# Eight rank-one products a batch in the low-rank layer become two products over four partitions

## The reference

```python
lt = x[:, 1:17, :]                      # sixteen tokens of each batch
even, odd = lt[:, ::2, :], lt[:, 1::2, :]
m1 = (even[:, :4, :, None] * odd[:, :4, None, :]).reshape(B, 512, 128)
m2 = (even[:, 4:, :, None] * odd[:, 4:, None, :]).reshape(B, 128, 512)
h = x @ W1.T + scale * einsum('bsd,bhd->bsh', x, m1) + b1
h = gelu(h)
out = h @ W2.T + scale * einsum('bsh,boh->bso', h, m2) + b2
```

## Time and profile before

| | |
|---|---|
| three timed executions | 821.05, 825.11 and 826.53 us, median 825.11 |
| the profiled execution | 825.88 us, of which the span from the first to the last instruction is 824.1 us |
| TensorE (PE) busy | 712.8 us (86%), mean granted clock 0.915 of full speed |
| VectorE (DVE) busy | 619.5 us (75%) |
| ScalarE (ACT), GpSimd (POOL) busy | 409.3 us, 394.3 us |
| fillers `ps_y<-zero_bf` within TensorE's time | 119.5 us |

### The profile page before, as it was taken

One profiled execution on the slowest core, in us unless ns is written; L12 is line 12 of the kernel. 1 busy time (PEld: TensorE's weight loads), 2 busy tenths in 40 slices (PEclk: granted clock), 3 DMA queues, 4 the chain that ended last, 5 costly groups with the idle time before them and its releaser, 6 DMA issues. The chain is left out here.

```text
span 824.1 us, 12171 instructions
## 1 busy us (share of the span) xinstructions
PE 712.8 (86%) x4422; PEld 423.6 (51%) x4422; DVE 619.5 (75%) x1083; ACT 409.3 (50%) x832; POOL 394.3 (48%) x475
## 2 busy tenths in 40 slices
PE   5468988997899888998899889997999889986867
PEld 2234545455645655555655655555655555554324
DVE  1277077998879866986989887988899778953692
ACT  1212633954397245843378248824682448433532
POOL 5543132694178413853269324962493018501671
PEclk9565999999999989996999999999999898967899
DMA  5321211431045101521054103520262114100410
GB/s 136 79 99 47 83 42 34 170 109 65 9 170 160 46 0 35 203 89 58 9 162 150 32 33 101 155 87 35 67 184 69 58 42 150 34 1 0 155 57 8
DMA packets 41241, 66.40 MB, mean 81 GB/s; under 512 B 8041, under 2 KB 30398, under 8 KB 38846
## 3 DMA queue, kind: packets, MB, share of 16 engines
q1 hardware_dynamic: 39006, 64.58, 24.4%
q10 hardware_dynamic: 2176, 1.05, 0.4%
HBM read 57.68 MB, written 7.86 MB: 80 GB/s over the span
## 5 line engine op out<-in xcount | busy, mean ns | idle before, releaser
L586 POOL TENSOR_TENSOR shared<-u,bcrow 128x512 f32<-128x512 f32 x128 | 203.6, 1620 | 64.1 <-DMA bcrow<-bc_dram 34.3
L963 DVE TENSOR_TENSOR_SCAN shared<-ps_f,shared 128x512 f32<-128x512 f32 x128 | 151.1, 1208 | 11.8 <-ACT ps_f L733 7.1
L865 DVE TENSOR_REDUCE mx<-ps_s 128x2 f32<-128x512 f32 (+1 forms) x192 | 126.0, 686 | 38.5 <-PE ps_s L1005 34.3
L1005 PE MATMUL ps_s<-stack_mem 72*128 72x128 bf16 (+3 forms) x1024 | 143.7, 260 | 7.7 <-DVE mx L865 5.6
L1005 PE MATMUL ps_y<-shared,ident 128*128 128x512 f32 (+1 forms) x288 | 121.8, 553 | 8.8 <-DVE shared L972 8.0
L733 ACT ACTIVATE ps_f<-delta,amat 128x255 f32<-128x255 f32 x256 | 109.8, 475 | 28.3 <-DVE shared L963 28.2
L1005 PE MATMUL ps_y<-zero_bf 128*128 128x512 bf16 x419 | 119.5, 409 | 1.9 <-DVE zero_bf L806 1.1
L1005 PEld LDWEIGHTS ps_s<-stack_mem 74*128 74x128 bf16 (+1 forms) x1024 | 83.8, 102 | 63.0 <-DVE mx L865 19.4
L670 ACT ACTIVATE probs<-ps_s 128x512 f32<-128x512 f32 x192 | 104.7, 595 | 22.7 <-PE ps_s L1005 22.1
L551 POOL TENSOR_TENSOR rstd<-mv,cst 128x2 f32<-128x2 f32 x32 | 6.2, 195 | 185.3 <-DVE mv L786 185.3
L972 DVE TENSOR_TENSOR shared<-shared,bcrow 128x1024 f32<-128x1024 f32 x56 | 78.9, 1409 | 1.8
(11 more groups left out here) (213 smaller groups left out, 1063.4 us busy)
## 6 DMA issues: line engine op xcount, KB each, us to landing
bcrow<-bc_dram SPq DMA_DIRECT2D x64, 512.0 KB, 4.2
stack_mem<-stack_dram SPq DMA_DIRECT2D x96, 192.0 KB
stack_dram<-parts SPq DMA_DIRECT2D x24, 256.0 KB, 4.5
x_tm<-in_L_attn_x_dram ACTq DMA_DIRECT2D x8, 128.0 KB, 2.1
xb<-in_L_attn_x_dram SPq DMA_DIRECT2D x8, 128.0 KB, 2.2
out_dram<-y_out SPq DMA_DIRECT2D x8, 128.0 KB, 4.8
fmem<-in_L_attn_conv_w_dram SPq DMA_DIRECT2D x1, 512.0 KB
lmem<-in_L_ffn_W_dram SPq DMA_DIRECT2D x2, 256.0 KB
```

The costliest lines, as they stand in the source:

```text
L586: G.tensor_tensor(bx[:, j % 2, c], u[:, c].unsqueeze(1).to_broadcast([P, 2, T]), bcrow[:, j % RING, 0], ALU.mult).then_inc(bx_sb, 1)
L865: V.tensor_reduce(mx[:, a, min(i, 1), hd[0]:hd[-1] + 1:2], ps_s[:, n % 2].rearrange("p (h n) -> p h n", h=len(hd)), AX.X, ALU.max).then_in ...
L963: V.tensor_tensor_scan(hs[:, j % HB, c].rearrange("p n t -> p (n t)"), ps_f[:, c, :], bx[:, j % 2, c].rearrange("p n t -> p (n t)"), 0.0, ...
L1005: return nc.tensor.matmul(o, lhsT, rhs, start=start, stop=stop, **kw)
```

## The change

The rows are laid out over four partitions. `lodd` is 4 x 2 x 128: on partition p the odd row of product p of `m1`, then that of `m2`. `ldiag` is 4 x 2 x 4 x 128: on partition p the even row of product p stands in the p-th quarter, for `m1` and for `m2`, and the other three quarters are zero. One matmul of `lodd[:, i]` (weights, 4 x 128) with `ldiag[:, i]` (4 x 512) then gives all four products at once, each in its quarter, since only one partition is not zero there. The zeros are written once, by a new memset of VectorE in `setup`.

The rows come by six DMAs instead of one: two for `lodd` (four partitions to four) and four for `ldiag` (two partitions to one). All add 16 to `lr_r`, and the first product waits for all six.

```diff
+LROWS = 16 * (LR + 2)
...
-        lrow = lmem[0:1, 0:LO]
+        lodd = lmem[0:LR, 0:2 * D].rearrange("p (i n) -> p i n", i=2)
+        ldiag = lmem[0:LR, LO // 2:LO].rearrange("p (i q n) -> p i q n", i=2, q=LR)
...
                 sp.wait_ge(x3_sb, b + 1)
-                sp.dma_start(lrow, x3[1:1 + 4 * LR, 0, :]).then_inc(lr_r, 16)
+                for i in range(2):
+                    sp.dma_start(lodd[:, i], x3[2 + 2 * LR * i:2 + 2 * LR * (i + 1):2, 0, :]).then_inc(lr_r, 16)
+                for p in range(LR):
+                    sp.dma_start(ldiag[p:p + 1, :, p], x3[1 + 2 * p:1 + 4 * LR:2 * LR, 0, :]).then_inc(lr_r, 16)
...
+                V.memset(lmem[0:LR, LO // 2:LO], 0.0)
                 V.tensor_scalar(inWg[:], inWg[:], rmsw[:, 0:1], None, ALU.mult)
...
                     if i == 0:
-                        pe.wait_ge(lr_r, b * 16 + 16)
+                        pe.wait_ge(lr_r, (b + 1) * LROWS)
                         pe.wait_ge(lr_sb, b + 1)
                     elif not is_last(b):
                         pe.wait_ge(weff, b * 2 + 1)
-                    for p in range(LR):
-                        even, odd = (lrow[:, (2 * (LR * i + p) + k) * D:(2 * (LR * i + p) + k + 1) * D] for k in range(2))
-                        last = mm(lo[i][:, p * P:(p + 1) * P], odd, even)
-                    last.then_inc(lo_ps, 1)
+                    mm(lo[i], lodd[:, i], ldiag[:, i].rearrange("p q n -> p (q n)")).then_inc(lo_ps, 1)
```

## The result

The changed kernel is slower by 3.7%: 853.71 us median (852.16 to 860.27, 4 runs) beside 825.62 us (821.05 to 826.53), 28 us more by the medians; the ratio of the means is 1.0367, with a 95% interval of 1.0299 to 1.0435. Run again on the chip of a later group it took 861.19 us beside 826.18, ratio 1.0442 (1.0387 to 1.0496). The profiled execution took 860.27 us, with a span of 858.5 us; it is the slowest of the first four, so its 34.4 us over the span before are more than the medians' 28.

The account below looks back on a forecast made before the run. A chain from engine to engine between x3 and the next scan was taken as the bound. Copies less products +10.1 us and clock +2 us made +12 on 825.9, or 838, stated as 837 us against the runs' median; range 826 to 848.

Parts of the forecast that it names:

- The copies: Six DMA issues on SyncE's queue instead of one: products 2.3 us later, TensorE stalls 15.2 us in all, +10.1 with products.
- The landing: Time from the end of a copy's issue until its rows have landed: 1.24 us, taken from the old copy.
- The slack: Between copy and first products, only three of eight batches can absorb delay: 1.43, 1.47 and 0.33 us.
- 0.8 of a stall passes on: Share of TensorE's net stall ahead of the products that lengthens the kernel: 0.8 x (15.2 - 2.5) = +10.1 us.
- The clock: Longer TensorE idle ahead of the products of batches 3 and 4 may lower its clock: +2 us, ends 0 and +8.
- a rival of +12: Longer waits throw TensorE's clock to half in batches 0, 3 and 4, 4 us each: 847 us; chance 0.12.
- The products: Groups of low-rank matmuls on TensorE take 1.02 us at full clock, not 1.15: -2.5 us if all on the path.
- The queue behind: Six DMAs to stack_mem behind the copy on SyncE's queue are issued about 2.5 us later: counted as nothing.
- The turning point of +8.2 us: Boundary between "not slower (within 1%)", chance 0.33, and slower; 1.8 us a copy would reach it with the clock's 2 us.
- the faster rival with cheap copies: Fewer small matmuls keep the clock up in batches 1, 2 and 6, -12 us; over 1% faster (815) has chance 0.03.
- The memset: VectorE's zeroing in setup takes a microsecond or so, hidden by a 2.46 us wait for ScalarE: costs nothing.
- The rule against the trace: Skill's rule that DMA issues cost little would give -2.5 us at most; the trace row, followed instead, says 1.2 later at least.

Follow-up runs that it names:

- the two queues: Changed kernel with three of the six copies issued by ScalarE and three by SyncE: 859.95 us, ratio 1.0423.
- the wide fillers: Kernel before with zero matmuls ahead of the first products and of other TensorE waits between x3 and the scan: 811.95 us, ratio 0.9824.
- the narrow ones: Kernel before with 1, 1, 4 and 6 more zero matmuls ahead of the first products of batches 1, 5, 6 and 7: 815.46 us, ratio 0.9894.
- the earlier copy: Kernel before with its copy issued once the first half of x3 is written: 821.67 us, ratio 0.9980; with further zero matmuls too, 812.41 us.

## Why the prediction was wrong

The direction and the place were right; the time lay outside the range, above it.

- **The copies** were the deciding term, as said, and mis-sized. I took 0.35 us a step for the `lodd` copies and 0.55 for `ldiag`, 2.3 us in all. The steps in the last batch were 0.64 to 0.70 and 0.60 to 0.64. I had split them by whether a copy folds partitions into one; the trace shows no gain for those that don't, and the copies from four partitions to four, of 2 KB, were even the dearer. The rows that I had called cheap and small carry 16 and 32 KB, so size doesn't make the difference either; they go to or from memory. The starts were later by 2.9 to 3.0 us where nothing gave slack, at the upper end that I had given (3.0), and 20.3 us in sum, against 15.2 taken and 20.8 as the end.
- **The landing** I had at 1.24 us behind the last issue; it was 1.55 - 0.56 = 1.0.
- **The slack** of batches 0, 2 and 3 was as read: their starts moved by 1.5, 1.5 and 2.6 us, the others by 3.0.
- **0.8 of a stall passes on.** With the clock held by fillers it was about 0.7; in batches 2, 5 and 6, where the clock hardly moved, all of it. This step stood, as roughly as it was meant.
- **The clock** is the step that failed. I gave it +2 us beside the stalls, 0 to +8 as ends, and a rival of +12 a chance of 0.12. Six long groups against two, 1.1% held back by fillers before and 2.7 to 3.4% after, put it at 11 to 19 us, and the growth of the batches beyond their later starts at 14 us. What misled me was to allow a fall in one batch, 3 or 4, where the clock fell further in batches 0, 1, 3, 4 and the tail. In batches 2 and 6, which had a low clock before already, nothing more was lost by it, and there I was right to count nothing. And I took the last batch of the kernel before, with 1.37 us of wait and full-speed products, as evidence that the clock bears such waits. The products came too soon to show it: they ended at 811.2, and from 812.1 to 815.4 the clock was 0.50.

```profile
812.10:815.40 3.30, 3.30 (x10) 1.95 (x8) 0.00 (x0) 0.84 (x2) 0.00 (x0) 0.50 0.02 5
```

With 20.3 us of later starts and the rival's 12 us, my own working gives 0.8 x (20.3 - 2.5) + 12 = +26 us, or 851.
- **The products** were to save 2.5 us at most. A group took 1.12 us, not 1.02, against 1.15, and 2.07 against 2.07 at half the clock. Two runs put the saving at nothing that can be told from zero. This puts 2 us back on my sum.
- **The queue behind** cost nothing that shows, as said: in neither profile does an engine wait for the fills of `stack_mem`, and the waits for the copy behind them (`stack_mem<-max_dram`) are 0.5 and 0.7 us of TensorE in all.
- **Two slips in the rivals' sums.** The turning point of +8.2 us comes at 1.7 us a copy by my own terms, not 1.8, and the faster rival with cheap copies at 817 us, not 815. Neither moves the forecast.
- **The memset** took 0.91 us, and the wait behind it shrank from 2.46 us to 0.64; free, as said:

```profile
50.77 0.91 DVE L833 MEMSET lmem<- 4x1024 f32 x1 [0.16 <-PE ps_s L1011]
...
55.51 1.98 DVE L871 TENSOR_REDUCE mx<-ps_s 128x4 f32<-128x512 f32 x3 [0.64 <-ACT wdT L622]
```

- **The rule against the trace.** That a sequencer's time to start a DMA is small beside the DMA itself (the Trainium skill, page "DMA: Bandwidth & Descriptors", section "Issuing engines are not separate DMA queues") doesn't hold for these copies: 0.56 of 1.55 us for the last of them, and 3.2 us of the 4.8 from the first issue to the products are issues of the five ahead.
- **The clock rule.** The Trainium skill, page "TensorE: Matmul & The Clock Gate", section "Part 1: The HAM clock gate", has throttled as the default and activity as what releases it. I had said that it would have this rival come true more often than not. The fillers' runs agree: zeros kept the clock at 1.00 in the first products of all eight batches of the changed kernel.

Left open: how much of the slow landing of the two queues is due to the `stack_mem` fills, and whether the wide fillers are better than the narrow ones. Nor does the length of a wait alone say whether the clock falls: batch 3 kept it through 2.52 us, and with three copies batch 1 through 1.37 us, when the group of batch 4 ran at 0.54 behind 1.10 us. (Batch 2 of the changed kernel is no case of it: its clock was at 0.50 before its wait of 2.38 us began.) And the two fastest runs of the changed kernel, at 852 us, had a mean clock of 0.914 over the whole run, no lower than the 0.915 of the kernel before; no profile of them was kept, so where their clock was low isn't known, and the 11 us of the lower end may be less.

## What to carry to other kernels

Before one copy is split into several to save matmuls, count the issues: they stand in a row on one queue, and what waits for the last waits for all of them. And when a wait of TensorE grows by two or three microseconds, the wait is only the first part of the price: look at the duration of the same matmuls on either side of such waits in the trace, and price the stretch behind at half the clock. The cheapest repair is to give TensorE something to do: a dozen matmuls of zeros in the waits made the kernel before faster by 1.1% (815.5 us). More of them, in other waits too, gave 1.8% (812.0 us), and 1.3% together with the earlier copy, which can't be told from 1.1%.

## What the runs showed of the hardware

- A copy from SBUF to SBUF held SyncE's queue for 0.56 to 0.63 us, at 1 KB and at 2 KB, from two partitions or four, as at 8 KB from sixteen (0.55; these are medians), while copies of 16 KB from memory and 32 KB to it had 0.26 and 0.30. From two queues at once each took 0.57 us or more, and one took 1.18.
- The same later starts cost less where TensorE is kept busy ahead of them: 5.9 us cost 14 us without fillers, and 6.9 us cost about 5 with them.
- The clock can fall behind the work that follows a wait, and not only in it: the products of batch 0 ran at 1.00 after a wait of 1.42 us, and the next 10 us at 0.50.
- Two matmul instructions with 4 x 512 operands took 1.12 us at full clock and 2.07 us at half, against 1.15 and 2.07 for eight with 1 x 128: the time of a group went with its columns (512 in either case), and hardly with the rows or the number of instructions.
